# One decoder layer in a single launch: six output pairs copied by ScalarE, ternary weights made by VectorE in slots

## The reference

```python
x = layernorm(x + attn(x))            # 16 heads of 128, causal, ALiBi, RMS norms on q, k and y
x = layernorm(x + xattn(x, ctx))      # 16 heads, compressed keys and values (64), rotary part (64), mask
x = layernorm(x + ffn(x))
# ffn, all three products:
def quant_weight(w):                  # 1024 x 256 each: gate, up, down
    scale = mean(abs(w)) + 1e-5
    return clip(round(w / scale), -1, 1) * scale
def quant_act(x):
    scale = max(max(abs(x), axis=-1), 1e-5) / 127
    return clip(round(x / scale), -128, 127) * scale
h = sigmoid(bitlinear(x, w_gate)) * bitlinear(x, w_up)
out = bitlinear(h, w_down)
```

## Time and profile before

| | us |
|---|---|
| median of 3 runs (1533.57 to 1535.42) | 1534.07 |
| the profiled execution | 1534.9 |
| its span, first to last instruction | 1532.9 |
| one steady tile of cross-attention (eight slots) | 46.0 |
| start of the feed-forward products | 1402.45 |

### The profile page before, as it was taken

How to read it: one execution, slowest core, us unless ns; L and a number is a source line. 1 busy time by engine, 2 the same in 40 slices (tenths; PEclk the granted TensorE clock), 3 DMA queues, 4 the chain that set the end, 5 groups by cost and what they waited for, 6 DMA issues and landing times. The chain is left out here.

```text
span 1532.9 us, 54215 instructions
## 1 busy us (share of the span) xinstructions
PE 1429.3 (93%) x20034; PEld 1053.8 (69%) x20034; DVE 1197.4 (78%) x2828; ACT 1262.6 (82%) x4046; POOL 1230.6 (80%) x1196
## 2 busy tenths in 40 slices
...
DMA packets 58372, 71.67 MB, mean 47 GB/s; under 512 B 14561, under 2 KB 42529, under 8 KB 58113
## 3 DMA queue, kind: packets, MB, share of 16 engines
...
## 5 line engine op out<-in xcount | busy, mean ns | idle before, releaser
L440 DVE SCALAR_TENSOR_TENSOR X<-projP,r,X 128x256 f32<-128x256 f32 x512 | 211.2, 475 | 2.7 <-PE projP L257 2.5
L237 PEld LDWEIGHTS svP<-W,xT 128*128 128x128 bf16 x3072 | 182.3, 98 | 30.5 <-issue 0.3
L208 PE MATMUL qkssP<-xT,W 128*128 128x512 bf16 x768 | 189.8, 384 | 13.5 <-POOL W L508 11.0
L503 POOL TENSOR_TENSOR y_sql<-y_sq 128x512 bf16<-128x512 f32 x128 | 133.2, 1041 | 79.0 <-ACT y_sq L324 78.6
L237 PE MATMUL svP<-W,xT 128*128 128x128 bf16 x3072 | 192.6, 219 | 0.2 <-issue 0.2
L208 PE MATMUL kP<-xT,W 128*128 128x512 bf16 x768 | 187.0, 380 | 0.0
L257 PE MATMUL projP<-W,y 128*128 128x256 bf16 x1024 | 177.1, 275 | 3.2 <-POOL yl L503 3.2
L339 ACT ACTIVATE probs<-scores,ntop 128x64 f32<-128x64 f32 x512 | 170.4, 339 | 2.3 <-DVE ntop L430 2.0
L1079 ACT ACTIVATE x_probs<-xsP,x_ntop 128x64 f32<-128x64 f32 x512 | 152.7, 326 | 18.9 <-DVE x_ntop L1153 18.1
L793 POOL TENSOR_TENSOR qhl<-qh 128x1024 bf16<-128x1024 f32 x64 | 121.3, 1895 | 42.1 <-issue 35.5
L503 POOL TENSOR_TENSOR k_sql<-k_sq 128x512 bf16<-128x512 f32 x128 | 133.3, 1042 | 22.4 <-ACT k_sq L344 21.8
...
## 6 DMA issues: line engine op xcount, KB each, us to landing
x_turned<-x_turn SPq DMA_DIRECT2D x128, 128.0 KB, 2.1
oB<-oA SPq DMA_DIRECT2D x256, 64.0 KB, 2.0
...
```

The costliest lines, as they stand in the source:

```text
L208: last = nc.tensor.matmul(dst[:, :], weight(parity, u, i, c), xT[:, z, c, tok], start=(c == 0 and k == 0), stop=(c == CC - 1 and k == 2))
L237: last = nc.tensor.matmul(svP[:, b * D:(b + 1) * D], xT[:, u, c, t * TILE + b * P:t * TILE + (b + 1) * P], weight(parity, z, 2, c), start= ...
L440: last = nc.vector.scalar_tensor_tensor(acc, projP[:, b * C:(b + 1) * C], r[:, PB + b:PB + b + 1], acc, ALU.mult, ALU.add)
L503: return nc.gpsimd.tensor_tensor(dst[:, :], src[:, :], high(src, slice(None), 0, TILE), ALU.subtract)
```

## The change

The ACT, PE and DVE work on the weights in slots 64 to 71 is removed. In its place DVE alone works on the weights in six halves of 128x1024:

- slots 8 to 12 and 16: one `tensor_reduce` of absolute values each (L1217 of the new kernel);
- slot 18: PE adds the six sums over the partitions through `xoP` (step "ws"), and DVE copies them out and makes the scale and two thresholds, +0.5 and -0.5 times it, in five small instructions;
- slots 20, 24, ... 64: one `scalar_tensor_tensor` each, two per half. The first (L1234) is max(w, lower) != w, the second (L1237) is (w > upper) - first. Both read two tensors in SBUF. They stand last in DVE's slot.

Pairs 58 to 63 (slots 65 to 70) are no longer copied to `oA` and sent by transfers. ACT copies the four 64x256 blocks from `xoP` straight to the rows of `oB` (L1102). It first waits until the output product of pair m - 2 has read that buffer (`s_proj`), and POOL waits for ACT in place of the transfers.

```diff
     S_AT, NORM_AT, T_AT, PTL_AT, PV_AT, PROJ_AT = 3, 4, 5, 6, 7, 9
     LAST = N + 2 * HP + 3
-    WEIGHTS_AT = N
+    DIRECT = N - 6
+    CHUNKS = 2 * 3
+    SUM_AT, SCALE_AT = (8, 9, 10, 11, 12, 16), 18
+    TERNARY_AT = tuple(range(20, 20 + 4 * 2 * CHUNKS, 4))
...
         j, g = divmod(n, HP)
+        if n == SCALE_AT:
+            return "ws", 0, 0
...
+        return sum(kind not in (None, "kr", "ws") for kind in STEPS[:n])
+
+    def reads_before(n):
+
+        return STEPS[:n].count("kr") + STEPS[:n].count("ws")
+
+    def chunk(k):
+
+        third, half = k % 3, k // 3
+        return slice(third * CC * DFF + half * DFF, third * CC * DFF + (half + 1) * DFF)
...
-                if has(n, PV_AT):
+                if has(n, PV_AT) and n - PV_AT < DIRECT:
                     m = n - PV_AT
...
                 wait(pe, s_oe, min(max(n - PV_AT + 1, 0), N))
                 wait(pe, s_out, outs_before(n))
-                wait(pe, s_kturn, turns_before(n))
+                wait(pe, s_read, reads_before(n))
...
+                elif kind == "ws":
+                    wait(pe, late["s_abs"], CHUNKS)
+                    last = nc.tensor.matmul(oP[:, 0:CHUNKS], kept["ones"][:, :], late["w_sums"][:, :], start=True, stop=True)
...
                 other(n)
-                if n == WEIGHTS_AT + 3:
-                    wait(pe, late["s_abs"], 3)
-                    wait(pe, s_lat, N)
-                    nc.tensor.matmul(latP[:, 0:3], kept["ones"][:, :], late["w_sums"][:, :], start=True, stop=True).then_inc(s_sum, 1)
...
                 if has(n, PV_AT):
                     m = n - PV_AT
                     wait(act, s_o, m + 1)
-                    wait(act, s_ot[m % 2], 64 * (m // 2))
-                    nc.scalar.activation(oA[:, m % 2].rearrange("p i (b t) -> p b i t", b=PB), oP[:, :].rearrange("p (b i t) -> p b i t", b=PB, i=2),
-                                         ACT.Copy).then_inc(s_oe, 1)
+                    by_head = oP[:, :].rearrange("p (b i t) -> p b i t", b=PB, i=2)
+                    if m < DIRECT:
+                        wait(act, s_ot[m % 2], 64 * (m // 2))
+                        nc.scalar.activation(oA[:, m % 2].rearrange("p i (b t) -> p b i t", b=PB), by_head, ACT.Copy).then_inc(s_oe, 1)
+                    else:
+                        wait(act, s_proj, m - 1)
+                        for par in range(2):
+                            for i in range(2):
+                                rows = oB[i * KVC:(i + 1) * KVC, m % 2, par * HT:(par + 1) * HT].rearrange("p (b t) -> p b t", b=PB)
+                                last = nc.scalar.activation(rows, by_head[par * KVC:(par + 1) * KVC, :, i, :], ACT.Copy)
+                        last.then_inc(s_oe, 1)
...
-                k = n - WEIGHTS_AT
-                cols = CC * DFF
-                if 0 <= k < 3:
-                    wait(act, late["s_ffn"], 3 * 16)
-                    nc.scalar.activation(ffn["flat"][k], late["okv"][:, k * cols:(k + 1) * cols], ACT.Abs,
-                                         accum_out=late["w_sums"][:, k:k + 1]).then_inc(late["s_abs"], 1)
-                if 4 <= k < 7:
-                    w = late["okv"][:, (k - 4) * cols:(k - 3) * cols]
-                    wait(act, s_winv, 1)
-                    nc.scalar.activation(w, w, ACT.Identity, bias=ffn["magic"][:, :], scale=winv[:, k - 4:k - 3]).then_inc(s_wm, 1)
...
-                k = n - WEIGHTS_AT
-                cols = CC * DFF
-                if k == 4:
-                    wait(dve, s_sum, 1)
-                    nc.vector.tensor_scalar(wsc[:, :], latP[:, 0:3], 1.0 / (C * DFF), EPS, ALU.mult, ALU.add).then_inc(s_wsc, 1)
+                okv = late["okv"]
+                if n in SUM_AT:
+                    k = SUM_AT.index(n)
+                    wait(dve, late["s_ffn"], 3 * 16)
+                    nc.vector.tensor_reduce(late["w_sums"][:, k:k + 1], okv[:, chunk(k)], AX, ALU.add, apply_absolute_value=True).then_inc(late["s_abs"], 1)
+                if kind == "ws":
+                    wait(dve, s_step, steps_before(n + 1))
+                    nc.vector.tensor_copy(sums[:, :], oP[:, 0:CHUNKS]).then_inc(s_read, 1)
+                    wait(dve, s_read, reads_before(n + 1))
+                    nc.vector.tensor_tensor(wsc[:, :], sums[:, 0:3], sums[:, 3:CHUNKS], ALU.add).then_inc(s_wsc, 1)
                     wait(dve, s_wsc, 1)
-                    nc.vector.reciprocal(winv[:, :], wsc[:, :]).then_inc(s_winv, 1)
-                if 5 <= k < 8:
-                    w = late["okv"][:, (k - 5) * cols:(k - 4) * cols]
-                    wait(dve, s_wm, k - 4)
-                    nc.vector.tensor_scalar(w, w, MAGIC, 1.0, ALU.subtract, ALU.min).then_inc(s_wr, 1)
-                    wait(dve, s_wr, k - 4)
-                    nc.vector.tensor_scalar(ffn["flat"][k - 5], w, -1.0, None, ALU.max)
+                    nc.vector.tensor_scalar(wsc[:, :], wsc[:, :], 1.0 / (C * DFF), EPS, ALU.mult, ALU.add).then_inc(s_wsc, 1)
+                    wait(dve, s_wsc, 2)
+                    nc.vector.tensor_scalar(cuts[:, 0, :], wsc[:, :], 0.5, None, ALU.mult).then_inc(s_cuts, 1)
+                    nc.vector.tensor_scalar(cuts[:, 1, :], wsc[:, :], -0.5, None, ALU.mult).then_inc(s_cuts, 1)
+                if n in TERNARY_AT:
+                    k, part_ = divmod(TERNARY_AT.index(n), 2)
+                    w, out_ = okv[:, chunk(k)], ffn["flat"][k % 3][:, k // 3 * DFF:(k // 3 + 1) * DFF]
+                    upper, lower = (cuts[:, i, k % 3:k % 3 + 1] for i in range(2))
+                    if part_ == 0:
+                        wait(dve, s_cuts, 2)
+                        nc.vector.scalar_tensor_tensor(out_, w, lower, w, ALU.max, ALU.not_equal).then_inc(s_below, 1)
+                    else:
+                        wait(dve, s_below, k + 1)
+                        nc.vector.scalar_tensor_tensor(out_, w, upper, out_, ALU.is_gt, ALU.subtract)
...
                 if has(n, PROJ_AT):
                     m = n - PROJ_AT
-                    wait(pool, s_ot[m % 2], 64 * (m // 2 + 1))
+                    if m < DIRECT:
+                        wait(pool, s_ot[m % 2], 64 * (m // 2 + 1))
+                    else:
+                        wait(pool, s_oe, m + 1)
                     wait(pool, s_proj, m - 1)
                     low_of(nc.gpsimd, oBl[:, m % 2, :], oB[:, m % 2, :]).then_inc(s_ol, 1)
```

More of the change, by code:

```diff
@@ L631, in cross_weights @@
             "tabs": tabs, "mask": mask, "s_mask": sem("l_mask"), "seg": seg, "segf": segf, "keys": keys, "loads": loads,
-            "s_weights": s_w, "weights": 9 * 16, "s_seg": s_seg, "s_segf": sem("l_segf"), "s_square": sem("l_square"), "s_ffn": sem("l_ffn"), "s_abs": sem("l_abs"), "w_sums": sb("w_sums", [P, 3], F32)}
+            "s_weights": s_w, "weights": 9 * 16, "s_seg": s_seg, "s_segf": sem("l_segf"), "s_square": sem("l_square"), "s_ffn": sem("l_ffn"), "s_abs": sem("l_abs"), "w_sums": sb("w_sums", [P, 6], F32)}
 def start_cross(nc, a, norm, ident, late, sem, own, kept):
@@ L856, in cross_attention @@
     moments, rstd2, xinv = sb("ln2_moments", [P, NB, 2], F32), sb("ln2_rstd", [P, NB], F32), sb("xinv", [P, NB], F32)
-    winv = sb("winv", [P, 3], F32)
+    sums, cuts = sb("sums", [P, 6], F32), sb("cuts", [P, 2, 3], F32)
     def ps(name, n=TILE):
@@ L869, in cross_attention @@
     s_swap, s_ot = [sem("c_swap0"), sem("c_swap1")], [sem("c_ot0"), sem("c_ot1")]
-    s_out, s_kturn, s_kadd, s_kmoved, s_ln1 = (sem("c_" + n) for n in ("out", "kturn", "kadd", "kmoved", "ln1"))
+    s_out, s_read, s_kadd, s_kmoved, s_ln1 = (sem("c_" + n) for n in ("out", "read", "kadd", "kmoved", "ln1"))
     s_low_ctx, s_xl, s_qcl, s_kl, s_KVl, s_xs = (sem("c_" + n) for n in ("lowctx", "xl", "qcl", "kl", "KVl", "xs"))
     s_stats, s_mom, s_ln, s_root, s_ln2, s_max, s_sc, s_xinv = (sem("q_" + n) for n in ("stats", "mom", "ln", "root", "ln2", "max", "sc", "xinv"))
-    s_sum, s_wsc, s_winv, s_wm, s_wr = (sem("q_" + n) for n in ("sum", "wsc", "winv", "wm", "wr"))
+    s_wsc, s_cuts, s_below = (sem("q_" + n) for n in ("wsc", "cuts", "below"))
     s_ctx = late["s_ctx"]
@@ L898, in outs_before @@
     def outs_before(n):
-        return sum(kind not in (None, "kr") for kind in STEPS[:n])
-    def turns_before(n):
-        return STEPS[:n].count("kr")
+        return sum(kind not in (None, "kr", "ws") for kind in STEPS[:n])
[4 more added lines that the diff above has]
+        return slice(third * CC * DFF + half * DFF, third * CC * DFF + (half + 1) * DFF)
     with nc.Block() as block:
@@ L936, in _ @@
                 if step(n)[0] == "kr":
-                    wait(sp, s_kturn, turns_before(n + 1))
-                    wait(sp, s_kadd, turns_before(n))
+                    wait(sp, s_read, reads_before(n + 1))
+                    wait(sp, s_kadd, step(n)[2] - 1)
                     sp.dma_start(moved_k[0:R, :], turned_k[R:P, :]).then_inc(s_kmoved, 16)
@@ L1048, in copy_out @@
                 kind, c, tile = step(n)
-                if kind in (None, "kr"):
```

(1 more changed line is left out.)

9 lines of the change are left out of this document (4 added, 5 removed).

## The result

The changed kernel takes 1561.09 us (median of 4 runs, 1557.32 to 1563.63) against 1534.74 of the kernel before on the same chip (4 runs, 1533.57 to 1537.88): ratio 1.0168, 95% interval 1.0152 to 1.0185. The forecast was 1552.6 in a range of 1543 to 1558; the change costs 26.4 us, not 18.5. Its profiled execution took 1561.67 us, with a span of 1558.6.

A forecast was written before the change was run, and what follows sets the result against it. Bound: each slot's cycle of ACT's exponentials, PE's scores and DVE's row maximum. Terms 0.7 + 1.7 + 7.0 + 9.05 + 1.1 = 19.5 us, less 1 for overstated cover, 18.5: 1552.6 us, range 1543 to 1558.

The forecast's parts named there:

- The main loop: Cross-attention before the tail: steady tile 48.8 us instead of 46.0, row maximum about 16 us late from slot 61 on.
- The sums: Six reductions in slots 8 to 12 and 16: 0.7 us in all, bounds 0 and 2.0.
- The scale: Slot 18's five small DVE instructions, the second waiting for POOL's `qhl`: +1.7 us, bounds 0.9 and 2.2.
- Ternary at g = 4: Slots 20, 28, ... 60: no turn to wait for, 1.14 to 1.2 us each, 7.0 in all, bounds 5 and 7.8.
- At g = 0: Slots 24, 32, ... 64: DVE mostly waits for POOL's instruction; 9.05 us in all, bounds 2.5 and 10.
- The races: Slots 32 to 56: POOL begins `qhl` 0.03 to 0.06 us ahead; if DVE won, costs of 1.6 to 2.3 become 0.1 to 0.8.
- Rival A: DVE loses no turn to POOL: scale costs 0.9 us, g = 0 costs 2.5, total 1546 us; chance 0.24.
- B: Turns cost more: late POOL stretches following slots, 0.5 us more at each of twelve places, 1559 us; chance 0.11.
- The 1.5 us wait at g = 5: DVE's wait for PE's key product, one slot after g = 4, does not help, standing behind the same exponentials.
- The tail: Last slots with direct copies: copies of pair 63 begin 4.3 us later, 3.2 regained after; net +1.1, bounds -4 and +4.
- The ring: Tail slots: copies wait for the output product of pair m - 2, next value product for copies; 3.6 us a slot.
- Rival C: Slots 65 to 71: copies do not wait for the output product, slots of 2.8 us, 1530 us in all; chance 0.05.

The follow-up runs named there:

- e1: Changed kernel with all 64 pairs sent by transfers, weights work kept in DVE's slots; 18.3 us over the kernel before.
- e8: e1 with the ternary instructions in the slots of e4, each moved ahead of DVE's wait there; 11.7 us over the kernel before.
- e4: Changed kernel with its twelve ternary instructions in slots of g = 4 and 5 (20, 21, ... 60, 61); 19.0 us over the kernel before.
- e15: Changed kernel plus matmuls that compute nothing needed, in PE's waits of slots 65, 66 and 68 to 71; 17.0 us over the kernel before.
- e12: Changed kernel with four row buffers in turn and `x_pth` ahead of the copy from slot 65; 13.4 us over the kernel before.
- e11: e2 with four row buffers in turn and `x_pth` ahead of the copy from slot 65; 3.4 us over the kernel before.
- e5: e2 with four row buffers in turn, so a copy waits for the output product four pairs earlier; 3.3 us over the kernel before.
- e2: Kernel before with only the last six pairs copied directly, weights work left where it was; 10.1 us over the kernel before.

## Why the prediction was wrong

- **The main loop: right.** Up to the row maximum of slot 64 the terms make 0.7 (sums) + 1.7 (scale) + 7.0 + 8.05 (ternary without slot 64's 1.0) - 1 = 16.4; measured 15.8 in the changed kernel, 16.1 in e1.
- **The sums: right.** Slots 8, 9 and 10 grow by 0.48, 0.37 and 0.22, slots 11, 12 and 16 shrink by 0.17, 0.02 and 0.02: 0.86 against 0.7 (0.57 in e1).
- **The scale: right.** Slot 18 takes 6.84 instead of 5.09, +1.75, and the wait of the second instruction is in its row.
- **Ternary at g = 4: right.** 1.27 us each; slots 20 to 60 grow by 1.1 to 1.2. **At g = 0: right in size and in the wait for POOL's end**, 2.90 to 3.04 us, slots +1.7 on the mean of slots 24 to 56. Who gets the turn was wrong in slot 24: POOL won although DVE's record begins first, +1.75 for the 0.8 taken. The races that it called decided by 0.03 to 0.06 us went as forecast, and were not as close as it thought, since 0.07 us in DVE's favour did not win slot 24. Slots 19 to 63 together lose 13.9 where 15.05 stood, since the slot behind each ternary instruction gives back some 0.1 and slot 55 0.35. Rival A (1546) is excluded by these rows, B too: the next slots give back time and do not stretch. That B's 1559 comes near 1561 is chance.
- **The 1.5 us wait at g = 5 "does not help": partly wrong.** Ahead of the wait an instruction costs 0.73 and not 1.1; POOL's `qhl` fills the gap (e8).
- **The tail: the step that failed.** The forecast was +1.0 (slot 64) and +1.1 with bounds -4 and +4, the +4 for "PE's clock in its lower level for some of it". Measured: +11.0. The ring and what hangs on it were named rightly: copies wait for the output product of pair m - 2, and the last step is 3.0 us shorter (3.2 forecast). Two sizes were not right. A slot is 3.9 at the high clock, not 3.6, and the loop with `x_pth`, `x_ptl` and the transposes in it is 5.74, which makes the copy of pair 63 late by 6.5 (e4) and 7.7 (e15) at a nearly full clock, not 4.3. The larger one is the clock, 7 to 8 us of the 14.9. The forecast put it at nothing in its value and at some 3 us in its upper bound, for some of the slots. In fact the direct copies make PE wait more, the clock falls, and a lower clock lengthens a ring in which PE's products are terms. Held up, the tail costs +3.8 (e15), inside the bounds; left alone, +11.0 in the changed kernel. The copies of slots 69 and 70, forecast 3.6 apart, start 5.2 and 3.9 behind the ones before them.
- **Rival C** (copies that do not wait for the output product) got its direction right in the tail of e12, -3.1; it never had the main loop.

The Trainium skill, GPSIMD Engine Reference, section Specifications, says that the two engines contend when DVE has two SBUF inputs; L384 gave the price. The trace agrees with both: e8 against e4, 2.34 against 1.28 us.

Open: what tips the clock, and with it how much of e4's shorter tail comes from where its last instructions stand; why e11's tail (57.11) is no shorter than e5's (55.83); and how much of the spread of the direct kernels' runs (1542.7 to 1549.5 in e2) is the moment at which the clock falls; one profile a kernel does not tell it.
